# NGCF graph convolution: adjacency blocks built in half-block units, with minima and centring on GpSimd and the compared iota in PSUM

## The reference, cut to what matters

```python
def conv(x, W1, W2, src, dst, n):               # n = 6250 nodes, 200000 edges, D = 64
    deg_out = clip(segment_sum(ones, src, n), 1.0)
    deg_in  = clip(segment_sum(ones, dst, n), 1.0)
    norm = rsqrt(deg_out[src] * deg_in[dst])
    msg = (x[src] @ W1 + x[src] * x[dst] @ W2) * norm[:, None]
    return x @ W1 + segment_sum(msg, dst, n)

h = maximum(layernorm(x), 0)                     # mean and variance over the 64 features
h = relu(conv(h, W1_1, W2_1, src, dst, n))
h = conv(h, W1_2, W2_2, src, dst, n)
out = x + h                                      # dst is sorted
```

## Time and profile before

| | us |
|---|---|
| median of 3 runs (lowest, highest) | 596.28 (594.68, 596.79) |
| the profiled execution's own time | 596.65 |
| its span | 594.8 |
| VectorE busy | 476.1 (80%) |
| TensorE busy | 513.5 (86%) |
| ScalarE busy | 276.9 (47%) |
| GpSimd busy | 49.1 (8%) |
| mean granted TensorE clock | 0.980 |

### The profile page before, as it was taken

The page is one execution under the profiler, slowest core; times in us unless marked ns, Lnnn a source line. Parts: engine busy times, 40 slices in busy tenths (PEclk is TensorE's granted clock), DMA queues, the critical chain, the costliest instruction groups (busy, mean ns, idle before and its releaser), DMA issues.

```text
span 594.8 us, 19344 instructions
## 1 busy us (share of the span) xinstructions
PE 513.5 (86%) x7970; PEld 462.2 (78%) x7970; DVE 476.1 (80%) x1217; ACT 276.9 (47%) x830; POOL 49.1 (8%) x43
## 2 busy tenths in 40 slices
PE   0277877778688888987999999999999999999996
PEld 0055655556566666766999999999989999999995
DVE  4588999999999999968877878778766666666663
ACT  0446876767789999863323232332321111111111
POOL 3696403000000000000000000000000000000000
PEclk9997999999999999996999999999999999999999
DMA  2175101000000000000000000000000011002010
GB/s 65 51 110 102 42 1 39 6 9 12 2 19 2 16 5 15 6 3 2 2 3 3 2 2 3 3 2 3 3 3 2 2 20 20 3 3 37 2 25 16
DMA packets 19428, 9.89 MB, mean 17 GB/s; under 512 B 16081, under 2 KB 18657, under 8 KB 19342
## 3 DMA queue, kind: packets, MB, share of 16 engines
q1 hardware_dynamic: 18222, 5.93, 5.5%
q0 software_dynamic: 1120, 2.72, 1.9%
HBM read 5.19 MB, written 1.65 MB: 11 GB/s over the span
## 4 chain that ended last, share of the span: by engine, by line
DVE 40%; PE 29%; ACT 14%; issue 10%; POOL 3%; DMA 3%; DVEq 0%; ACTq 0%; POOLq 0%
PE diff L728 23%; DVE los L448 15%; DVE mixed L506 7%; ACT hots L768 4%; ACT words L778 2%; ACT h L844 2%; DVE work L595 2%; PE diff L712 2%; DVE hots L453 2%; DVE work L573 2%; PE slab L675 2%; ACT h L801 2%; DVE work L579 2%; DVE work L582 2%; POOL late L354 1%
## 5 line engine op out<-in xcount | busy, mean ns | idle before, releaser
L675 PEld LDWEIGHTS slab<-hots,los 128*128 128x128 bf16 x2352 | 123.3, 99 | 79.1 <-DVE hots L453 64.0
L675 PE MATMUL slab<-hots,los 128*128 128x98 bf16 x2352 | 137.2, 210 | 44.3 <-DVE hots L453 44.2
L448 DVE TENSOR_TENSOR los<-mixed,iota_p 128x6144 bf16<-128x6144 bf16 x49 | 164.3, 3352 | 0.6 <-PE slab L675 0.4
L728 PE MATMUL diff<-los,mixed 128*128 128x129 f16 x2401 | 159.4, 222 | 4.1 <-DVE los L554 3.5
L728 PEld LDWEIGHTS diff<-los,mixed 128*128 128x128 fp8e4 x2401 | 153.1, 101 | 6.2 <-issue 3.6
L728 PE MATMUL diff<-late,mixed 128*128 128x128 f16 x2401 | 150.7, 219 | 1.1 <-DVE late L598 1.1
L728 PEld LDWEIGHTS diff<-late,mixed 128*128 128x128 fp8e4 x2401 | 145.6, 98 | 2.0 <-DVE late L598 0.7
L768 ACT ACTIVATE hots<-diff 128x784 bf16<-128x784 f32 x147 | 128.5, 902 | 39.4 <-PE diff L646 38.7
L506 DVE TENSOR_SCALAR mixed<-words 128x400 int32<-128x400 int32 x294 | 89.8, 361 | 0.0
L646 PE MATMUL diff<-select,mixed 80*128 80x392 f16 x294 | 76.2, 342 | 5.2 <-DMA mixed<-rows 4.3
L778 ACT ACTIVATE words<-slab 128x400 uint16<-128x400 uint16 x98 | 53.5, 546 | 7.8 <-PE slab L675 5.1
(11 more groups left out here) (118 smaller groups left out, 443.1 us busy)
## 6 DMA issues: line engine op xcount, KB each, us to landing
mixed<-rows SPq DMA_DIRECT2D x147, 12.0 KB, 1.8
x_sb<-in_x_dram SPq DMA_DIRECT2D x4, 384.0 KB
out_dram<-x_sb SPq DMA_DIRECT2D x8, 128.0 KB
los<-in_dst_dram SPq DMA_DIRECT2D x1, 750.0 KB
out_dram<-x_sb SPq DMA_DIRECT2D x4, 80.0 KB
out_dram<-x_sb SPq DMA_DIRECT2D x4, 48.0 KB
los<-samples,row_i POOLq DMA_INDIRECT x7, 2.5
late<-in_src_dram,begin_i POOLq DMA_INDIRECT x7, 6.0
```

Source lines behind the costliest of these rows:

```text
L448: nc.vector.tensor_tensor(out=los[:, b % 3].rearrange("e s (v t) -> e s v t", t=2), in0=key, in1=val, op=ALU.is_equal).then_inc(los_ready, 1)
L675: ins = nc.tensor.matmul(both, los[:, b % 3, step], hots[:, b % 2, :, step, 0:BLOCKS], start=False, stop=(j == 8 * STEPS - 1))
L728: ins = nc.tensor.matmul(acc[a][:, 0:width], tiles[:, a, q], parts[:, q, 0:width], start=(q == 0), stop=(q == BLOCKS - 1))
```

## The change

Blocks are built in 98 units of half a block (24 steps). `low_hots`, the minima, the products and the saving of words all go by units; `los` is a ring of 6 units and `hots` one of 4 (the same bytes as before). The bf16 iota is copied once into a PSUM bank and compared from there. The minimum moves to GpSimd. The histogram is no longer saved by ScalarE and summed by TensorE: VectorE adds the slab's 49 columns to a sum in SBUF (`hist`), some units late (`hist_lag`, 5 at first and 2 from unit 42 on); `bias` is 392 columns wide. A weight matmul pair covers two consecutive steps that may lie in two units. The centring and the squares of the norm go to GpSimd, and 1/std with relu to VectorE in 7 pieces. The fetches are spread between GpSimd's minima and go to a place of their own for each tile.

```diff
+UNITS = 2 * BLOCKS
+USTEPS = BSTEPS // 2
+UPT = 2 * PER_TILE
-    los = sb("los", [128, 3, BSTEPS, 128], BF16)
-    hots = sb("hots", [128, 2, 2, BSTEPS, QW], BF16)
+    los = sb("los", [128, LOS_RING, USTEPS, 128], BF16)
+    hots = sb("hots", [128, HOT_RING, 2, USTEPS, QW], BF16)
-    hist_part = sb("hist_part", [128, 4, Q - 1], BF16)
+    hist = sb("hist", [128, Q - 1], FP32)
-    hist = ps("hist", [128, 512])
+    iota_bank = ps("iota_bank", [128, 512])
+    iota_pairs = iota_bank[:, 0:64]
+    iota_ps = iota_pairs.bitcast(BF16)
...
+    SAVE_AFTER = {UPT * t + 4: t + 1 for t in range(TILES - 1)}
+    TURN_AFTER = {UPT * t + 6: t + 1 for t in range(TILES - 1)}
+    KEYS_AFTER = {UPT * t + 7: t + 1 for t in range(TILES - 1)}
+    FETCH_AFTER = {4 + 2 * (t - 2) + k: (t, k) for t in range(2, TILES) for k in range(2)}
+    NORM_SUM, NORM_CENTRE, NORM_VAR, NORM_STD, NORM_RSTD, NORM_OUT = 18, 22, 27, 42, 45, 47
+    def hist_lag(u):
+        return max(2, 5 - u // UPT)
+    def slots(m):
+        return [((2 * m + i) // STEPS, (2 * m + i) % STEPS) for i in range(2)]
+    def pairs_of(u):
+        return (STEPS * (u + 1) + 1) // 2
+    def pairs_beside(u):
+        first = 3 * (u // 2) + 4
+        return [m for m in ((first, first + 1) if u % 2 == 0 else (first + 2,)) if m < UNITS * STEPS // 2]
...
 GpSimd
+            def ones_of(u):
+                pool.wait_ge(weights_ready, pairs_of(u))
+                nc.gpsimd.tensor_scalar(hots[:, u % HOT_RING, 1], hots[:, u % HOT_RING, 0], 1.0, None,
+                                        ALU.min).then_inc(hots_ready, 1)
+            def norm_part(i, step):
+                qs = slice(i * PIECE, (i + 1) * PIECE)
+                if step == 0:
+                    pool.wait_ge(summed, i + 1)
+                    p(nc.gpsimd.tensor_scalar(neg_mean[:, qs], row_sum[:, qs], -1.0 / D, None, ALU.mult))
+                    p(nc.gpsimd.tensor_tensor(out=h[:, qs], in0=x_sb[:, qs],
+                                              in1=neg_mean[:, qs].unsqueeze(2).to_broadcast([128, PIECE, D]),
+                                              op=ALU.add))
+                else:
+                    if i:
+                        pool.wait_ge(var_ready, i)
+                    nc.gpsimd.tensor_tensor(out=squares, in0=h[:, qs], in1=h[:, qs], op=ALU.mult).then_inc(squared, 1)
...
             pool.wait_ge(begin_ready, 2)
-            for t in range(1, TILES):
-                if t >= RING:
-                    pool.wait_ge(rows_ready, t - RING + 1)
-                fetch(t)
+            for k in range(2):
+                fetch(1, k)
+            for u in range(UNITS):
+                ones_of(u)
+                if u in FETCH_AFTER:
+                    fetch(*FETCH_AFTER[u])
+                if u >= NORM_CENTRE and u - NORM_CENTRE < 2 * (BLOCKS // PIECE):
+                    norm_part((u - NORM_CENTRE) // 2, (u - NORM_CENTRE) % 2)
...
 VectorE
+            nc.vector.memset(hist[:], 0.0).then_inc(hist_added, 1)
+            v(nc.vector.tensor_copy(iota_pairs, iota_p[:].bitcast(FP32)))
...
+            def low_hots(u):
+                steps = slice(u * USTEPS, (u + 1) * USTEPS)
+                dve.wait_ge(keys_ready, u // UPT + 1)
+                if u >= LOS_RING:
+                    dve.wait_ge(slab_ready, u - LOS_RING + 1)
+                key = keys[:, steps, :].unsqueeze(2).to_broadcast([128, USTEPS, 64, 2])
+                val = (iota_ps.rearrange("e (v t) -> e v t", t=2).unsqueeze(1)
+                       .to_broadcast([128, USTEPS, 64, 2]))
+                nc.vector.tensor_tensor(out=los[:, u % LOS_RING].rearrange("e s (v t) -> e s v t", t=2),
+                                        in0=key, in1=val, op=ALU.is_equal).then_inc(los_ready, 1)
+            def add_hist(u):
+                dve.wait_ge(slab_saved, u + 1)
+                dve.wait_ge(hist_added, u + 1)
+                nc.vector.tensor_tensor(out=hist[:], in0=slab[u % 2][:, HALF:HALF + BLOCKS], in1=hist[:],
+                                        op=ALU.add).then_inc(hist_added, 1)
...
+            for u in range(UNITS):
+                low_hots(u)
+                while added <= u - hist_lag(u):
+                    add_hist(added)
+                    added += 1
+                if u == 1:
+                    find_begin(1, TILES)
                 for part, decode in enumerate((decode_source, decode_place, decode_rows)):
-                    if b in DECODE_AFTER[part]:
-                        decode(DECODE_AFTER[part][b])
+                    if u in DECODE_AFTER[part]:
+                        decode(DECODE_AFTER[part][u])
...
+                norm_part(u)
             dve.wait_ge(slab_saved, 4)
+            dve.wait_ge(los_ready, UNITS)
+            dve.wait_ge(diff_ready, UNITS * STEPS // 2)
             unpack(0)
+            while added < UNITS:
+                add_hist(added)
+                added += 1
+            dve.wait_ge(hist_added, UNITS + 1)
+            nc.vector.tensor_scalar(rdo[:], hist[:], 1.0, None, ALU.max).then_inc(deg_ready, 1)
...
             unpack(1)
...
 TensorE
+            def products(u):
+                for m in pairs_beside(u):
+                    weigh_hots(m)
+                if u >= 2:
+                    pe.wait_ge(slab_saved, u - 1)
+                    pe.wait_ge(hist_added, u)
+                mine = slab[u % 2][:]
+                nc.tensor.matmul(mine[:, 0:HALF], sixteens[:], bias[:], start=True, stop=False, skip_group_check=True)
+                pe.wait_ge(los_ready, u + 1)
+                pe.wait_ge(hots_ready, u + 1)
+                for step in range(USTEPS):
...
 ScalarE
+            for u in range(UNITS):
+                for m in pairs_beside(u):
+                    save_weights(m)
+                if u in SAVE_AFTER:
+                    save_source(SAVE_AFTER[u])
+                if u in KEYS_AFTER:
+                    save_keys(KEYS_AFTER[u])
...
+                save_words(u)
```

More of the change, by code:

```diff
@@ L486, in second_scale @@
                 dve.wait_ge(bound_ready, 1)
-                v(nc.vector.tensor_reduce(out=bound[:], in_=bound_ps[:, 0:D], axis=AX.X, op=ALU.max))
+                v(nc.vector.tensor_reduce(out=bound[:], in_=bound_ps, axis=AX.X, op=ALU.max))
                 v(nc.vector.tensor_scalar(bound[:], bound[:], 2.0 ** -60, None, ALU.max))
@@ L637, in turn, with weigh_hots @@
                 ins.then_inc(turned, 1)
[L639 to L642 removed]
+            def weigh_hots(m):
                 if m >= 2:
                     pe.wait_ge(weights_ready, m - 1)
[L645 to L648 removed]
@@ L679, in _ @@
-            pe.wait_ge(consts, 12)
+                for bank, (u, k) in enumerate(slots(m)):
+                    i, t, j = u % 2, u // UPT, u // 2 % PER_TILE
+                    if i == 0 and k == 0:
+                        pe.wait_ge(stack_in[t % 2][j], 48 * (t // 2 + 1))
+                    ins = nc.tensor.matmul(diff[m % 2][:, bank, 0:HALF],
+                                           stack[0:80, t % 2, j, k * 128:(k + 1) * 128],
+                                           select[0:80, i * HALF:(i + 1) * HALF], start=True, stop=True)
@@ new lines, in weigh_hots @@
+                ins.then_inc(diff_ready, 1)
+            def products(u):
[9 more added lines that the diff above has]
+                for step in range(USTEPS):
+                    group = step // STEPS
+                    both = bass.AP(mine.tensor, mine.offset + group * BLOCKS,
+                                   [mine.ap[0], [HALF - group * BLOCKS, 2], [1, BLOCKS]])
+                    ins = nc.tensor.matmul(both, los[:, u % LOS_RING, step], hots[:, u % HOT_RING, :, step, 0:BLOCKS],
+                                           start=False, stop=(step == USTEPS - 1), skip_group_check=True)
+                ins.then_inc(slab_ready, 1)
@@ L680, in _ @@
+            pe.wait_ge(consts, 11)
             turn(0)
             pe.wait_ge(select_ready, 1)
[L682 to L692 removed]
@@ L693, in _ @@
-            add_hist(2 * BLOCKS - 1)
+            for m in range(4):
+                weigh_hots(m)
+            for u in range(UNITS):
+                products(u)
+                if u == BOUND:
+                    pe.wait_ge(wabs_ready, 1)
+                    pe.wait_ge(consts, 16)
+                    nc.tensor.matmul(bound_ps, norms, wabs, start=True, stop=True).then_inc(bound_ready, 1)
+                if u in TURN_AFTER:
+                    turn(TURN_AFTER[u])
+            pe.wait_ge(slab_saved, UNITS)
@@ L735, in _ @@
                         pe.wait_ge(totals_ready, 1)
[L736 removed]
+                        nc.tensor.matmul(sum_ps[0:1, 0:2], ones[:], totals[:], start=True,
                                          stop=True).then_inc(totals_summed, 1)
```

258 lines of the change are left out of this document (79 added, 179 removed).

## The result

| | before | changed |
|---|---|---|
| median, us (lowest, highest) | 596.53 (594.68, 597.54), 4 runs | 732.69 (731.98, 733.39), 4 runs |
| ratio, 95% interval | | 1.2287 (1.2252 to 1.2321) |
| span, us | 594.8 | 730.2 |
| GpSimd / VectorE busy, us | 49.1 / 476.1 | 356.5 / 538.4 |
| mean granted TensorE clock | 0.980 | 0.909 |

What follows compares the result with a forecast made beforehand. VectorE was taken to bound the kernel before 268 us, TensorE in the unchanged stage after. Gains 6.0 + 16.6 + 5.2 less 0.3, 8 and 3 made 16.5 us: 580 us, eight in ten from 564 to 604.

Steps and rivals of the forecast that it cites:

- GpSimd's load: Build stage: 98 minima at 1.2 us plus fetches and norm steps, 146 us, hidden in VectorE's some 205 us.
- Rival B: Build stage: GpSimd's minimum of m us becomes the bound above m = 2.07, kernel slower, 615 us; chance 0.13.
- rival C: Build stage: coupling and contention stretch the unit to 1.95 to 2.0 us, total 591 to 594 us; chance 0.14.
- Rival A: VectorE's comparison with its PSUM operand drops to one element at a time, 3.3 us a unit, total 726 us; chance 0.08.
- Steady state on VectorE: Build stage: minima and their idle time removed, less split comparisons, histogram additions and norm: net 16.6 us gained.
- Start-up: Before the old 46.51 us mark: GpSimd's indirect DMAs no longer held up by comparisons, 6.0 us gained, less 0.3.
- Contention the other way: VectorE's decode and 1/std instructions wait for GpSimd's minima: 8 us lost, at most 59.
- Coupling: Build stage: tight handovers between VectorE at 1.84 us and TensorE at 1.75 us a unit, 3 us lost (0 to 15).
- End of the stage: From last comparison to first scaled piece: 4.6 us instead of 9.8, 5.2 us gained.
- Multiply stage: The second stage, after the first scaled piece: untouched by the change, as long as before within 2 us.

Runs made afterwards that it cites:

- experiment 1: The changed kernel with its minima moved from GpSimd to VectorE, all else as changed: 606.12 us, ratio 1.0159.
- experiment 7: The changed kernel with minima on VectorE and the histogram copied by ScalarE and added by GpSimd: 592.42 us, ratio 0.9925; the second time 591.58 us, 0.9935.

## Why the prediction was wrong, step by step

**GpSimd's load: the step that failed.** I took 1.2 us for its minimum, "by the iota, the nearest in size", over a range of 0.9 to 2.7. Measured: 3.22 us start to start, above even the top. Both choices were unsound. Size was the wrong kinship: an iota and a memset read nothing, and the only row of a large instruction that reads a tensor was the select, whose proportional rate gave the 2.7. And the top took the select's fixed part as nothing, yet still fell short, so it was no bound at all but one more guess. The centrings came as taken, 972 ns for 1 us. The sentence "hidden" in 205 us rested on it.

**Rival B was right as a mechanism**, and got 0.13. Its formula, 29.9 + 28 + 98 m + 7, gives 382 us with m = 3.24; the first scaled piece came at 403, the rest being GpSimd's 22.7 us of waiting, less 2 us at the end. Its break-even of 2.07 us and the prices 619 and 658 were only as good as the range of m, and the time range of 604 left it out. One sum beside it was wrong: rival C gives m = 1.8 to 2.0 the same time as itself, 591 to 594, but by this formula the pieces then start at 241 to 261 us, which is 570 to 590.

**Rival A did not happen.** 726 us was near the measured 733 by accident; the comparison ran at 0.57 ns a column. A time that fits is no mechanism: the row decides. The Trainium skill, "VectorE: DVE Perf Modes", section "The perf-mode tier table", gives `tensor_tensor` with any PSUM operand the 1x rate, and the 1744 ns refute it for this form. The Trainium skill, "Vector Engine (DVE) Microarchitecture Reference", section 5.1, has a table of the modes; its line for two 16-bit results a cycle includes `tensor_tensor` and does not ask for SBUF; the trace agrees.

**Steady state on VectorE.** Comparison 1.67 us a unit (1.70 taken), additions at 0.12 spacing (0.14 taken), 205 ns recorded. But I subtracted whole minima from VectorE, and once they came back the remainder lost: experiment 1.

**Start-up.** Right where GpSimd was not yet bound: both fetches take 0.95 us and `find_begin` no longer waits. The data was then of no use, since the decode waited 13.92 us for GpSimd.

**Contention the other way.** Taken as 8 us from a minimum of 1.2. The seven decode rows sum to 89 us in place of 21, and the seven 1/std pieces to 11.2 in place of 4.3: 75 us of waiting, above the 59 I called the most. That bound took each to wait for one minimum of 1.2 us; a minimum was 3.24, and two instructions waited through more than four. Most of it lay in GpSimd's shadow; what came out of it is the 22.7 us.

**Coupling.** Taken as 3 us. In the changed kernel it is the path by which VectorE's waits reached GpSimd: TensorE stood 54.3 us behind VectorE's additions. What it costs by itself at the pace of 1.84 that I forecast was not tested. **End of the stage:** 4.5 us against my 4.6, seen in experiment 7, where GpSimd did not bound the stage. **Multiply stage:** 327.0 us against 326.6, unchanged.

## What to carry to other kernels

Before work goes to an engine that the trace shows only at small or write-only jobs, measure that very instruction there: the one missing price was the whole result, and a bound from other kinds of instruction is no bound. Give the idle slow engine the small work that costs the bound engine mostly fixed time (49 columns here), not the long streaming work. Where GpSimd computes, take one of the two inputs of VectorE's long instructions from PSUM if you can, and count the waits in both directions. One SBUF input alone is no safeguard: the longest waits fell on such an instruction.

## What the runs showed of the hardware

A GpSimd instruction of one tensor and a constant costs 2.7 ns a column (3.28 us for 1200), whatever the type or operation tried; of two tensors 1.8, a copy 1.0. VectorE compares two bf16 tensors at 0.54 ns a column with one of them in PSUM as in SBUF. A VectorE instruction that needs what GpSimd holds can be passed over by several GpSimd instructions in a row: 384 columns, 0.35 us of work, waited through more than four minima for 13.92 us, and in another tile for 14.17; in other stretches such instructions waited for one. What decides between the two is not shown. An indirect DMA's issue on GpSimd took up to 7.77 us beside a comparison with both inputs in SBUF, and 0.93 to 1.29 with one of them in PSUM.
